# A graph-network kernel on one core: the edge layer's bias products on 32 rows of TensorE's array

## What is computed

```python
hi = einsum('bsh,hk->bsk', x, W1[:H]); hj = einsum('bsh,hk->bsk', x, W1[H:])
h = relu(hi[:, :, None, :] + hj[:, None, :, :] + b1)
y = einsum('bijk,kl->bijl', h, W2) + b2
y = layernorm(y, gamma, beta)
out = einsum('bij,bijh->bih', adj, y)
```

## Time and profile before

| | |
|---|---|
| median of 3 runs | 462.51 us (462.26 to 462.81) |
| the profiled execution | 461.34 us |
| its span, first to last instruction | 459.6 us |
| PE busy | 436.0 us, 95%, 3427 matmuls |
| PEld busy | 413.2 us, 90% |
| DVE busy | 414.5 us, 90%, 1523 instructions |
| ACT busy | 386.6 us, 84% |
| POOL busy | 354.1 us, 77% |
| mean granted TensorE clock | 0.991 of full speed |

### The profile page before, as it was taken

The page is one execution under the profiler, slowest core; times in us unless marked ns, Lnnn a source line. Parts: engine busy times, 40 slices in busy tenths (PEclk is TensorE's granted clock), DMA queues, the critical chain, the costliest instruction groups (busy, mean ns, idle before and its releaser), DMA issues. The chain is left out here.

```text
span 459.6 us, 14156 instructions
## 1 busy us (share of the span) xinstructions
PE 436.0 (95%) x3427; PEld 413.2 (90%) x3427; DVE 414.5 (90%) x1523; ACT 386.6 (84%) x1003; POOL 354.1 (77%) x651
## 2 busy tenths in 40 slices
PE   3799989999999999999999999999999999999991
PEld 3699989999999999889998999999999999999991
DVE  5799999999999999996998898889889988988966
ACT  2378979999999899998798888888888888888973
POOL 5289979999999899745777687778777776868652
PEclk9999999999999999999999999999999999999996
DMA  6133345445445652233323131322222222313011
GB/s 221 41 105 111 93 151 161 156 137 182 148 148 164 213 190 89 65 116 113 122 70 99 53 102 52 88 66 76 78 70 84 65 89 62 92 51 98 24 49 48
DMA packets 50939, 47.60 MB, mean 104 GB/s; under 512 B 5584, under 2 KB 42576, under 8 KB 50896
## 3 DMA queue, kind: packets, MB, share of 16 engines
q1 hardware_dynamic: 49328, 46.16, 32.7%
q10 hardware_dynamic: 1568, 0.96, 0.7%
HBM read 28.22 MB, written 18.87 MB: 102 GB/s over the span
## 5 line engine op out<-in xcount | busy, mean ns | idle before, releaser
L1575 PEld LDWEIGHTS bank<-w2c,hE 128*128 128x128 f32 x512 | 67.3, 192 | 2.4
L1575 PE MATMUL bank<-w2c,hE 128*128 128x128 f32 x512 | 67.5, 275 | 0.0
L905 ACT ACTIVATE hE<-bank,front 128x512 f32<-128x512 f32 x64 | 44.3, 691 | 7.6 <-PE bank L1556 7.4
L925 ACT ACTIVATE sqE<-bank 128x512 f32<-128x512 f32 x63 | 37.7, 599 | 12.9 <-PE bank L1575 12.5
L1230 DVE TENSOR_REDUCE ssum<-sqE 128x4 f32<-128x512 f32 x63 | 42.7, 677 | 4.4 <-ACT sqE L925 2.9
L1097 DVE BATCH_NORM_STATS2 stats<-t 128x6 f32<-128x128 f32 x192 | 44.5, 273 | 1.5 <-issue 1.4
L703 POOL TENSOR_TENSOR gHl<-gH,gHu 128x512 fp32r<-128x512 f32 x32 | 41.1, 1285 | 5.7 <-ACT gHu L879 5.7
L1255 DVE TENSOR_TENSOR ym<-bank,wE 128x512 f32<-128x512 f32 x64 | 43.2, 682 | 1.6 <-POOL wE L752 0.3
L719 POOL TENSOR_TENSOR half<-ym 128x512 f32<-128x512 f32 x31 | 39.4, 1273 | 3.3 <-DVE ym L1255 3.1
L1606 PE MATMUL bank<-yC,ST 128*128 128x128 f32 x256 | 34.3, 277 | 3.1 <-ACT yC L944 3.1
L1573 PE MATMUL bank<-bias,ones_b 128*128 128x512 bf16 x96 | 36.5, 380 | 0.6 <-DVE ym L1255 0.6
(11 more groups left out here) (189 smaller groups left out, 1628.5 us busy)
## 6 DMA issues: line engine op xcount, KB each, us to landing
hh_scratch<-hh SPq DMA_DIRECT2D x32, 256.0 KB, 2.2
gH<-hh_scratch SPq DMA_DIRECT2D x32, 256.0 KB, 2.8
A<-adj_groups SPq DMA_DIRECT2D x32, 128.0 KB, 2.1
res_scratch<-res SPq DMA_DIRECT2D x32, 128.0 KB, 2.0
gRES<-res_scratch SPq DMA_DIRECT2D x32, 128.0 KB, 2.4
AT<-adjT_groups SPq DMA_DIRECT2D x30, 128.0 KB, 2.3
out<-y SPq DMA_DIRECT2D x30, 128.0 KB, 1.9
X<-x_groups SPq DMA_DIRECT2D x28, 128.0 KB, 2.2
```

What stands on the lines that cost most here:

```text
L905: nc.scalar.activation(hE[g][:, :], HE_ps, ACT.Relu, bias=C["L3_b1"]).then_inc(b[f"hE{g}_ready"], 1)
L925: nc.scalar.activation(sqE[g][:, :, :], YE_ps[g], ACT.Square).then_inc(b[f"sqE{g}_ready"], 1)
L1575: last = nc.tensor.matmul(ps[:, i, :], hidden[:, i * P:(i + 1) * P], w2c[:, :], start=False, stop=i == tiles - 1)
```

## The change

`bias3` gets another layout: partition 0 holds the first part of the bias, partition 1 the second, 2 the third, and the same again from partitions 32 and 64; the rest is zero. It is written on all 128 partitions: `first3` has three columns of zeros and ones, picked from the identity matrix (`first3[p, r]` is 1 for p = r, r + 32 and r + 64), and each part of the bias is multiplied by its column and added. The bias product of the edge layer then reads partitions 0 to 31 alone, of the ones and of `bias3`, as a tile of 32 rows and 128 columns at place (0, 0) of the array. The bias products of layers 0 and 1 stay as they are.

```diff
-        part = [sb(f"part{n}", [P, P], bf16) for n in range(6)]
+        part = [sb(f"part{n}", [P, P], bf16) for n in range(7)]
...
+        first3 = sb("first3", [P, 3])
...
             def split_layer3():
-                split_bias(b2c[:, :], bias3, ELL, 4)
+
+                for r in range(3):
+                    nc.vector.tensor_reduce(first3[:, r:r + 1], ident[:, r:3 * 32:32], AX.X, ALU.add)
+
+                def keep(r, part):
+                    if r == 0:
+                        return nc.vector.tensor_scalar(bias3[:, :, :], part.unsqueeze(1).to_broadcast([P, ELL, P]), first3[:, 0:1], None, ALU.mult)
+                    return nc.vector.scalar_tensor_tensor(bias3[:, :, :], part.unsqueeze(1).to_broadcast([P, ELL, P]), first3[:, r:r + 1], bias3[:, :, :], ALU.mult, ALU.add)
+
+                then(nc.vector.tensor_copy(part[4][:, :], b2c[:, :]))
+                nc.vector.tensor_tensor(split[0][:, :], b2c[:, :], part[4][:, :], ALU.subtract)
+                then(keep(0, part[4][:, :]))
+                then(nc.vector.tensor_copy(part[5][:, :], split[0][:, :]))
+                nc.vector.tensor_tensor(split[1][:, :], split[0][:, :], part[5][:, :], ALU.subtract)
+                then(keep(1, part[5][:, :]))
+                then(nc.vector.tensor_copy(part[6][:, :], split[1][:, :]))
+                keep(2, part[6][:, :]).then_inc(s_bias, 1)
...
             def project(ps, hidden, tiles, done):
-                nc.tensor.matmul(run(ps), ones_b[:, :], run(bias3[:, :, :]), start=True, stop=False)
+                nc.tensor.matmul(run(ps), ones_b[0:32, :], run(bias3[0:32, :, :]), start=True, stop=False, tile_position=(0, 0))
```

More of the change, by code:

```diff
@@ L1650, in graph @@
                         after(pe, "hT_ready", n)
-                        nc.tensor.matmul(run(aY_ps), ones_b[:, :], run(bias3[:, 0:TILES, :]), start=True, stop=False)
+                        nc.tensor.matmul(run(aY_ps), ones_b[0:32, :], run(bias3[0:32, 0:TILES, :]), start=True, stop=False, tile_position=(0, 0))
                         for i in range(TILES):
```

## The result

The changed kernel takes 492.85 us in the median (491.16 to 492.87, 4 runs) against 462.38 us beside it: a ratio of 1.0654, 95% interval 1.0631 to 1.0676, so 30.5 us slower. The forecast was 473.5 us. Its sign was right and its size wrong: 30 us where 11 were expected. The time lies in the wide range that was to hold 8 times in 10, at the place of rival 1, and outside the 466 to 482 us of the forecast's own mechanism.

A forecast was written before the change was run, and what follows sets the result against it. The prediction took TensorE's matmul order in the edge layer as the bound; 10.6 us for shape changes plus 0.4 for the split made 11.0, giving 473.5 us on the median's scale, with an 8-in-10 range of 461.6 to 496.

The forecast's parts named there:

- rival 1: Deep drain: both shape changes wait for the whole pass and write-back, 0.16 us each, 30.7 us, time 493.6; chance 0.28.
- the forecast's own mechanism: A short stop at the bias products' shape changes, 0.04 to 0.2 us a product, 466 to 482 us; chance 0.42.
- TensorE bounds the edge layer, so what is added to its order is added to the span: From 200 us on, each microsecond added to TensorE's order lengthens the span, less 0.9 us of idle time.
- Nothing saved by fewer rows: Bias products on 32 rows: streamed columns set the slot and the weight load is hidden, so 0 us saved.
- The price of a change of shape: 0.055 us at each, 0.11 a product: Around each bias product, the time to cross 128 rows charged at both changes: 96 x 0.11 = 10.6 us.
- a sign that its size is wrong: Around each bias product: the forecast is wrong in size if the first and second change don't cost alike.
- My reason for the low end: Price nearer nothing than 59 us, because loads ahead of fp32 products of another type show no gap.
- One sign that the prediction gave for it: At the bias products, with the deep drain: weight loads no longer start with the matmul ahead of them.
- with the loads exposed as well: Deep drain with the weight loads around each bias product also uncovered: 59 us, time up to 521.
- The split: 0 to 1.4 us, 0.4 taken: Vector's bias split at 59.8 to 63.4 us grows by 0 to 1.4 us; 0.4 us taken as reaching TensorE.
- two waits go: In Vector's bias split, two waits disappear with the new layout, counted in its new sum of 3.65 us.

The follow-up runs named there:

- twice128: The kernel before with each bias product issued twice in a row on the full array: 483.28 us, ratio 1.0451.
- rows96: The kernel before with the bias product on partitions 0 to 95 and no place in the array named: 462.26 us, ratio 0.9999.
- tile_only: The kernel before with the bias product on the 32-row tile at (0, 0) and the old split of the bias: 488.81 us, ratio 1.0581.
- tile64: The changed kernel with the bias product on a tile of 64 rows at (0, 0), parts written into the first quarter alone: 492.49 us, ratio 1.0639.
- twice32: The changed kernel with each bias product issued twice in a row, both on rows 0 to 31: 510.56 us, ratio 1.1056.
- merged_quarters: The changed kernel with a unit's three bias products issued together (26 of 32 units), on rows 0, 32 and 64, each with its own PSUM bank: 490.62 us.
- split_only: The kernel before with only the new way of splitting the bias on Vector, bias products on the full array: 463.9 us, ratio 1.003.
- after_again: The changed kernel measured and profiled once more, nothing changed: 491.61 us, ratio 1.0622.
- spread: The kernel before with its bias split cut into five pieces 3 us apart in Vector's plan: 464.14 us, ratio 1.0027.

## Why the prediction was right and wrong

*TensorE bounds the edge layer, so what is added to its order is added to the span.* Right. `twice128` adds 0.22 us a product, its slot, all of it in the time.

*Nothing saved by fewer rows.* Right: `rows96` is unchanged, and a second product adds 0.216 us to a unit on 32 rows and 0.218 on 128.

*The price of a change of shape: 0.055 us at each, 0.11 a product.* This is the step that failed. That the change of shape brings a stop is shown (`tile_only`, `rows96`, `tile64`, `twice32`), with the named place as the one thing left open; the term was mis-sized. It is 0.30 us a product by starts and 0.29 over the edge layer, where m0 hides some, against my 0.11. I took the pass through the array as the whole price and left the loads under cover: "the weights for the next shape can be held ready as they are now". In no profile here are they: across a change the load starts with its matmul, in both directions. Nor do the two changes cost alike, which the prediction had named as a sign that its size is wrong: 0.10 us going in, 0.20 going out.

What the 0.30 us are made of stays open. By size alone a bf16 load of 0.09 and an fp32 load of 0.19 are 0.28 of it. By place they don't all fit. In the 0.10 us ahead of the bias product its load can't be running, since it starts with the product and the loader is idle; and in `twice32` the first of two small products, whose load of 0.09 starts with it, holds the second back by only 0.01 by the records. A wait for the matmul before to leave the array fits the way in as well, and it is the same behind three kinds of product. `tile64` doesn't decide it: its load takes 0.09 us too, and its way in also starts from the full array. The ends of matmul records are modelled, and no run takes the loads away without the stop.

My reason for the low end, that loads run ahead across a change of type, was true and told nothing about a change of shape.

*Rival 1.* It came out at 493.6 us, 0.75 above the measured time, by two whole passes of 0.16 us. One sign that the prediction gave for it is there: the weight loads no longer start with the matmul ahead of them. But with the loads exposed as well it had 59 us, and its halves of 0.16 are not the measured 0.10 and 0.20. That the total comes so close is partly luck: its price of 30.7 us stands against 27.2 in the edge layer, and the split and the clock, for which it had 0.4, fill the gap.

The Trainium skill, in "TensorEngine Tiling (Array Packing)", section Key Properties, says that a change of tiling mode drains TensorE; that had the sign, and no run here shows a draining apart from the loads. The rule of its page "TensorE: Matmul & The Clock Gate", section "Part 3: Packing small matmuls", that loads overlap matmuls only where row groups differ is contradicted twice: full-row loads run ahead, and in `twice32` a load for rows 0 to 31 runs ahead of a matmul on rows 0 to 31. (The same section of the Trainium skill also lets loads go ahead where they fill a background weight buffer, and these rows don't contradict that.) The claim of the Trainium skill, in the same section, that tiles on different rows run at once agrees with `merged_quarters`, where three start 3 to 6 ns apart.

*The split: 0 to 1.4 us, 0.4 taken.* Low: it cost 1.4 us (`split_only`, 0.4 to 2.4 by its interval), the most that the prediction allowed, and not 0.4. That "two waits go" was misread: two go and three come, five `then` instead of four. Vector needs 4.57 us from 61.05 to 65.62 in the kernel after:

```profile
61.05 0.27 DVE L1083 TENSOR_REDUCE first<-ident 128x1 f32<-128x3 f32 x3
62.59 0.82 DVE L1087 TENSOR_SCALAR bias<-part,first 128x512 bf16<-128x512 bf16 x1
...
63.91 0.75 DVE L1088 SCALAR_TENSOR_TENSOR bias<-part,first,bias 128x512 bf16<-128x512 bf16 x1
...
65.62 0.42 DVE L1140 SCALAR_TENSOR_TENSOR unlike<-AT 128x256 bf16<-128x256 f32 x1
```

That is 0.95 us over before, and it goes on to TensorE, which is idle for 2.46 us between 60 and 72 us instead of 1.55. What the sum didn't hold is the clock: in the first profile the lower level in 68 to 72 us let only 20 matmuls through where 32 to 34 go at the higher one, some 1.7 us by its mean of 0.57. That agrees with the first bias product, at 195.1 us there and at 193.5 in `after_again`. Its place varies from run to run by more than the split costs: 190.8 to 193.6 us in the profiles with the old split (the last is `spread`, with a stretch at the lower clock), 191.5 to 195.3 in those with the new one.

The total nearly adds up: 26 to 27 us for the tile, 1.4 for the split and 1.6 for the stretches at the lower clock are 29.0 to 29.9 of 30.5 us; the rest is within the intervals of these numbers, and no run names it.

## What to carry to other kernels

Where TensorE has no gaps, a product on a tile of its own shape among full-array products costs some 0.3 us, more than its own 512 columns, so use one shape throughout. Tiles side by side on different rows can pay for the two changes: by the numbers here it takes three, and they were worth 0.22 us a unit in `merged_quarters`, where gathering them had cost 1.0 us a unit. Read starts and loads, not durations: the bias product's record grew by 6 ns while it cost 300. Before products are gathered to share such a change, look how long the banks that they fill are still being read.

## What the hardware showed that I had not expected

Weights for the shape that runs are loaded up to 0.22 us ahead; for another shape the load waits, from 128 rows to 32 or 64 and back alike, at 0.30 us for the pair of changes, 0.10 in and 0.20 out. Three 512-column products on rows 0, 32 and 64 took 0.39 us together. A longer pause of TensorE (2.46 us idle in one piece) was followed in one profile by 4 us at a mean clock of 0.57, and one of 2.48 us in `tile64` by a mean of 0.58; one of 2.47 us in `split_only` was followed by full clock. What decides it isn't shown.
